# Layer 4 of a fused four-layer graph network: 244 edge tiles without gathers in place of 148, the new ones three nodes wide in three PSUM banks

## What is computed

```python
edge_index = jnp.stack([src, dst])
...
h = jnp.maximum(_layernorm(x, axis=-1), 0.0)
x = x + _L2_gnn_ref(h, edge_index, L2_gnn_Wp, ...)
h = jnp.maximum(_layernorm(x, axis=-1), 0.0)
x = x + _L3_gnn_ref(h, L3_gnn_weight, L3_gnn_loop_weight, edge_weight1, src, dst, edge_type_8)
...
def _L3_gnn_ref(feat, weight, loop_weight, norm, src, dst, etypes):
    all_h = jnp.einsum('ni,rio->rno', feat, weight)
    msg = all_h[etypes, src] * norm
    h = jax.ops.segment_sum(msg, dst, num_segments=feat.shape[0])
    return h + feat @ loop_weight
```

## Time and profile before

| | us |
|---|---|
| median of 3 executions | 6198.45 (6195.6 to 6209.36) |
| profiled execution | 6148.6 |
| its span, first to last instruction | 6146.8 |
| PE busy in the span | 3852.7 (63%) |
| POOL busy | 3724.3 (61%) |
| DVE busy | 2867.0 (47%) |
| ACT busy | 1417.4 (23%) |

### The profile page before, as it was taken

One profiled execution on the slowest core, in us unless ns is written; L12 is line 12 of the kernel. 1 busy time (PEld: TensorE's weight loads), 2 busy tenths in 40 slices (PEclk: granted clock), 3 DMA queues, 4 the chain that ended last, 5 costly groups with the idle time before them and its releaser, 6 DMA issues.

```text
span 6146.8 us, 69225 instructions
## 1 busy us (share of the span) xinstructions
PE 3852.7 (63%) x20719; PEld 3015.9 (49%) x20719; DVE 2867.0 (47%) x9736; ACT 1417.4 (23%) x5476; POOL 3724.3 (61%) x3922
## 2 busy tenths in 40 slices
PE   4889999565555555555555588867466565565433
PEld 3455665454545545455544466634344444444332
DVE  7777776554545455555555533334322322222222
ACT  5333443332223233333333201122000000000000
POOL 4344443566666666666666466645666666666665
PEclk7799999766667677777777799979777777776666
DMA  3233443544444444444444455544111111111121
GB/s 110 95 117 132 145 142 116 157 136 139 137 136 142 135 137 140 146 139 139 138 150 137 147 201 204 192 142 178 47 46 47 46 47 46 46 46 46 47 62 47
DMA packets 310272, 707.07 MB, mean 115 GB/s; under 512 B 72641, under 2 KB 155293, under 8 KB 297613
## 3 DMA queue, kind: packets, MB, share of 16 engines
q0 software_dynamic: 159184, 377.89, 21.4%
q1 hardware_dynamic: 148700, 323.81, 15.2%
q10 hardware_dynamic: 2016, 0.92, 0.1%
HBM read 571.29 MB, written 131.05 MB: 114 GB/s over the span
## 4 chain that ended last, share of the span: by engine, by line
PE 32%; another core or an unknown queue 28%; DVE 19%; issue 15%; ACT 3%; DVEq 1%; DMA 1%; SPq 1%; ACTq 0%
PE ps L2586 11%; DVE oneh L1875 6%; PE ps L2542 4%; DVE ps L2010 3%; PE ps L2571 3%; PE ps L2481 3%; PE ps L2609 3%; PE ps L2493 2%; PE ps L2549 2%; DVE third L2002 2%; PE ps L2431 1%; DVE tmp L1966 1%; ACT h L1644 1%; PE ps L2545 1%
## 5 line engine op out<-in xcount | busy, mean ns | idle before, releaser
L1482 POOL DMA_INDIRECT rows<-tab_rel,third x1299 | 1251.0, 963 | 625.8 <-issue 371.8
L1482 POOL DMA_INDIRECT rows<-tab_hp,idx_src x1120 | 1083.4, 967 | 546.3 <-issue 310.5
L1482 POOL DMA_INDIRECT rows<-tab_h,idx_src x810 | 783.8, 968 | 777.0 <-PE ps L2549 432.5
L2609 PE MATMUL ps<-third 128*128 128x128 f32 x3126 | 618.8, 359 | 666.1 <-issue 416.8
L2586 PE MATMUL ps<-third,h 128*120 128x385 bf16 (+20 forms) x4606 | 875.8, 337 | 68.2 <-issue 29.8
L2609 PEld LDWEIGHTS ps<-third 128*128 128x128 f32 x3126 | 551.8, 264 | 721.4 <-issue 453.1
L2542 PE MATMUL ps<-oneh,rows 128*128 128x128 f32 x2598 | 484.6, 339 | 597.5 <-DVE oneh L1875 301.9
L2542 PEld LDWEIGHTS ps<-oneh,rows 128*128 128x128 f32 x2598 | 428.8, 244 | 682.5 <-issue 347.5
L2586 PEld LDWEIGHTS ps<-third,h 128*120 128x120 bf16 (+10 forms) x4606 | 588.2, 131 | 286.0 <-issue 59.3
L1693 ACT ACTIVATE turned_words<-turned_words 128x128 f32<-128x128 f32 x1563 | 463.1, 298 | 1117.3 <-DVE turned_words L2015 874.5
L1482 POOL DMA_INDIRECT third<-tab_hp,idx_src x443 | 430.2, 971 | 229.2 <-issue 120.8
(11 more groups left out here) (285 smaller groups left out, 5123.1 us busy)
## 6 DMA issues: line engine op xcount, KB each, us to landing
third<-dst_flat SPq DMA_DIRECT2D x390, 256.0 KB
h<-cnt_d SPq DMA_DIRECT2D x48, 1568.0 KB
cnt_d<-h SPq DMA_DIRECT2D x46, 1568.0 KB
tab_rel<-third SPq DMA_DIRECT2D x49, 512.0 KB
rows<-tab_rel,third POOLq DMA_INDIRECT x1299
rows<-tab_hp,idx_src POOLq DMA_INDIRECT x1120
rows<-tab_h,idx_src POOLq DMA_INDIRECT x810
third<-tab_hp,idx_src POOLq DMA_INDIRECT x443
```

The lines of the kernel that those rows point to most:

```text
L1482: pool.indirect_dma_start(out=to[:, t, 0:n], out_offset=None, in_=table[:, :], in_offset=bass.IndirectOffsetOnAxis(ap=idx[:, col:col + 1], ...
L2609: last = pe.matmul(ps_t[sl][:, t * P:(t + 1) * P], onehT[:, sl, t * P:(t + 1) * P], pwin[:, st["v"] % 2, :], start=True, stop=True)
```

## The change

The dense part takes 96 tiles more, 148 to 243, in packs of one tile. Their window is three nodes wide: `pairs3` has 49x3x8 = 1176 columns, `count3` makes three matmuls (408, 408, 360 columns) into three banks, which rotate over banks 0 to 3, and five packs (15 slots, 120 columns) make a bundle. So there are 20 bundles more, 33 in all. The heads move behind, to tiles 244 to 359 (still 116 gathers, but 26 heads), and the tiles gathered from `tab_rel` are 360 to 1562: 1203 in 301 turns. Each bank's eviction is signalled alone, and a count waits for its own bank only. The keys' rows stand in another part of SBUF. `WIN3` becomes a width per pack.

```diff
-PACKS3 = ((4, 36), (2, 76), (1, 148))
-WIN3, SLOTS3, NQ3 = 2, 16, 3
+PACKS3 = ((4, 36, 2), (2, 76, 2), (1, 148, 2), (1, 244, 3))
+SLOTS3, NQ3 = 16, 3
...
-HEAD_END, HEAD_WIN, HEAD_SPAN, HEAD_BATCH = 66, 16, 11, 4
+HEAD_END, HEAD_WIN, HEAD_SPAN, HEAD_BATCH = 90, 16, 11, 4
...
+    bundles3 = []
+    while not bundles3 or bundles3[-1][-1] < len(packs3) - 1:
+        k0 = bundles3[-1][-1] + 1 if bundles3 else 0
+        w = packs3[k0][2]
+        bundles3.append([k for k in range(k0, min(len(packs3), k0 + SLOTS3 // w)) if packs3[k][2] == w])
...
+                            n_banks = -(-nb * w // 512)
+                            per_bank = -(-nb // n_banks)
+                            parts = []
+                            for q0 in range(0, nb, per_bank):
+                                bank = next(bank_at) % 4
+                                parts.append((bank, q0, min(nb, q0 + per_bank), n_cev3.get(bank, 0)))
...
-                pack_cost = 1.1 * (nt3 * 1700.0 + len(bundles3) * (nb * 400.0 + 2000.0))
+                pack_cost = 1.1 * (sum((t1 - t0) * 850.0 * w for t0, t1, w in win3_runs) + len(bundles3) * (nb * 400.0 + 2000.0))
...
-                    for b, (q0, q1) in enumerate(((0, st["half"]), (st["half"], nb))):
-                        last = act.copy(weights3[:, q0:q1, st["place"]:st["place"] + w3],
-                                        ps[st["bank"] + b][:, 0:(q1 - q0) * w3].rearrange("p (q c) -> p q c", c=w3))
-                    last.then_inc(s_cev3.handle, 1)
+                    w = st["w"]
+                    for bank, q0, q1, _ in st["parts"]:
+                        act.copy(weights3[:, q0:q1, st["place"]:st["place"] + w],
+                                 ps[bank][:, 0:(q1 - q0) * w].rearrange("p (q c) -> p q c", c=w)).then_inc(s_cev3.handle, 1)
...
-                    if st["free"]:
-                        pe.wait_ge(s_cev3.handle, st["free"])
-                    for b, (q0, q1) in enumerate(((0, st["half"]), (st["half"], nb))):
-                        last = pe.matmul(ps[st["bank"] + b][:, 0:(q1 - q0) * w3], srow3[:, slot, :],
-                                         pairs3[:, slot, q0 * w3:q1 * w3], start=st["start"], stop=st["stop"])
+                    w = st["w"]
+                    for bank, q0, q1, evicted in st["parts"]:
+                        if st["start"] and evicted:
+                            pe.wait_ge(s_cev3.handle, evicted)
+                        last = pe.matmul(ps[bank][:, 0:(q1 - q0) * w], srow3[:, slot, :],
+                                         pairs3[:, slot, q0 * w:q1 * w], start=st["start"], stop=st["stop"])
```

More of the change, by code:

```diff
@@ L138, in gnn_program @@
                 if u == 0 or forms[u - 1] != forms[u]]
-    packs3 = [(t, n) for k, (n, end) in enumerate(PACKS3) for t in range(PACKS3[k - 1][1] if k else 0, end, n)]
-    pack3_of = {t0 + j: k for k, (t0, n) in enumerate(packs3) for j in range(n)}
-    per3 = SLOTS3 // WIN3
-    bundles3 = [list(range(k, min(len(packs3), k + per3))) for k in range(0, len(packs3), per3)]
-    w3 = WIN3 * n_rel
+    packs3 = [(t, n, w) for k, (n, end, w) in enumerate(PACKS3) for t in range(PACKS3[k - 1][1] if k else 0, end, n)]
+    pack3_of = {t0 + j: k for k, (t0, n, w) in enumerate(packs3) for j in range(n)}
+    bundles3 = []
[3 more added lines that the diff above has]
+        bundles3.append([k for k in range(k0, min(len(packs3), k0 + SLOTS3 // w)) if packs3[k][2] == w])
+    bundle3_of = {k: u for u, members in enumerate(bundles3) for k in members}
+    win3 = [packs3[members[0]][2] for members in bundles3]
+    win3_runs = []
+    for k, (n, end, w) in enumerate(PACKS3):
+        if win3_runs and win3_runs[-1][2] == w:
+            win3_runs[-1] = (win3_runs[-1][0], end, w)
+        else:
+            win3_runs.append((PACKS3[k - 1][1] if k else 0, end, w))
+    w3 = max(win3) * n_rel
+    col3 = nth + 4
+    total3 = col3 + len(bundles3)
+    assert total3 < 512
     full_tiles = n_edges // P
@@ L2197, in vector_keys3_rows @@
             k = t = 0
-            for n, end in PACKS3:
+            for n, end, _ in PACKS3:
                 m = (end - t) // n
@@ L2243, in vector_keys3_keys @@
             idx, u_rel, u_blk, u_row = (tmp_words[:, k * nt3:(k + 1) * nt3].bitcast(U32) for k in range(4))
-            f_rel, f_blk, f_key, f_in = (tmp_words[:, k * nt3:(k + 1) * nt3] for k in range(4, 8))
+            f_rel, f_blk, f_key, f_in = (tmp_words[:, k * nt3:(k + 1) * nt3] for k in (4, 5, 0, 1))
             dve.wait_ge(s_idx3.handle, 16)
@@ L2467, in tensor_program @@
                     for u, members in enumerate(bundles3):
-                        n = len(members) * WIN3
-                        last = pe.matmul(ps[3][0:n, 320 + u:321 + u], first_col[:, u * SLOTS3:u * SLOTS3 + n], ones[0:1, 0:1],
+                        n = len(members) * win3[u]
+                        last = pe.matmul(ps[3][0:n, col3 + u:col3 + u + 1], first_col[:, u * SLOTS3:u * SLOTS3 + n], ones[0:1, 0:1],
                                          start=True, stop=True)
@@ L2473, in tensor_program @@
                     pe.wait_ge(s_key3.handle, st["rows"] + 3)
-                    pe.matmul(ps[3][:, 384:385], ones[:, :], n_inside3[:, :], start=True, stop=True).then_inc(s_key3T.handle, 1)
+                    pe.matmul(ps[3][:, total3:total3 + 1], ones[:, :], n_inside3[:, :], start=True, stop=True).then_inc(s_key3T.handle, 1)
                 elif kind == "count3":
```

78 lines of the change are left out of this document (45 added, 33 removed).

## The result

The changed kernel takes 6164.11 us (median of six executions, 6158.85 to 6177.85); the kernel before, on the same chip, 6202.86. The ratio is 0.9942, 95% interval 0.9931 to 0.9954: 0.6% or 36 us faster (28 to 43); the plain medians lie 39 us apart. The prediction was 6144 us with a range of 6070 to 6360.

A forecast was written before the change was run, and what follows sets the result against it. Layer 4 was taken to run at its gathers' pace, 1.433 us each. 6148.6 - 137.6 (96 gathers) + 58 (X) + 13 + 2 (keys) + 10 (heads) = 6094; plus 49.9 from profile to median, 6144 us; range 6070 to 6360.

The forecast's parts named there:

- the sign: Layer 4's dense part after the change: 1.47 to 1.52 us per gather, clock over 0.85, PE about 85% busy.
- The keys' rows: Small DVE operations that PE and layer 3's gathers wait for: +13 us, all taken as on the path.
- the heads: 13 more adds and three more batches before layer 4's gathers: +10 us, between 0 and 24.
- X: What the new dense work costs layer 4's gathers: +58 us, from 872 gathers at 1.5 us in place of 1.433.
- a bundle has 29.4 us of such work in 37.9: Dense part: PE's full-rate work per bundle, 29.4 us, fits in 37.9 us of gathers; 78% overall.
- Rival B: PE becomes the dense part's bound and the change costs time: 6232 or 6362 us, X from 112 on; chance 0.35.
- sparse stretches: Within the products, single PE instructions 0.70 us apart with nothing to wait for; 8.9 us idle per bundle, 293 for 33.
- Rival A: PE's added work costs the gathers nothing, X under 20: 6091 us, or 6061 with keys and heads hidden; chance 0.18.
- the factor of 1.45: PE's busy time over its full-rate work in the old dense part, 811.0 us for 561, at clock 0.74.
- C: The effects cancel: X between 100 and 125, time 6186 to 6211 us; chance 0.09.
- D: Tiles that don't fit their three nodes start the general loop; left out, as none of 148 to 243 spans more.
- by its rate of instructions: Bound for X from the matmul instruction rate of 3600 to 3900: 7314/5.12 = 1429 us, +179.

The follow-up runs named there:

- pairs_other_form: Changed kernel with DVE writing each pair matrix by scalar_tensor_tensor in place of tensor_scalar: 6183.42 us, ratio 0.9968 to the kernel before, first chip (before about 6203 us).
- three_together: Changed kernel with pairs_other_form's instruction, two-node windows to tile 196 and batched keys' rows: 6137.74 us, ratio 0.9891 to the kernel before, first chip.
- few_products: Changed kernel whose 20 new bundles do 2 of their 49 products each: 5391.6 us, ratio 0.9863 to the kernel before, second chip (before 5461 to 5467 us).
- tiles_248: Changed kernel with 100 new tiles in place of 96, filling the last bundle: 5392.01 us, ratio 0.9865 to the kernel before, second chip.
- two_nodes_to_196: Changed kernel with the first 48 new tiles two nodes wide in two banks, not three: 5373.49 us, ratio 0.9831 to the kernel before, second chip.

## Why the prediction came out as it did

**The direction and the main terms were right.** 1203 gathers, the dense part at 1.50 to 1.53 us per gather (1.47 to 1.52 was named as the sign), clock 0.95 for "over 0.85", PE 86% busy for 85%. The keys' rows cost 13.1 us for 13; the heads 6 for 10, within 0 to 24; the restructuring nothing.

**X was mis-sized: 58 in the sum, 87 by the trace.** With 87 and 6 in their places the sum gives -30 in place of -54; the measured ratio says 36, with 28 to 43 as the interval. The 58 was a choice between bounds, from the pace of another stage, and named no mechanism of its own, so that it came near 87 is partly luck. POOL's longer waits for PE alone are 75. A second cost, the 28 us of longer issues, the prediction put at nothing. It asked of DVE only whether it would be late, with 100 us more of pair matrices, and it wasn't. But while such an operation runs, POOL's issue beside it is longer, and POOL's issue is the pace itself. The rows for it stood there: the issues have a mean of 927.98/958 = 0.969 us in the dense part of the first trace, and a minimum of 0.938. The Trainium skill has the mechanism ("SBUF — State Buffer", section "SBUF: two separate sides"): VectorE and GpSimd share a pair of ports, which a VectorE operation in a two-port mode holds for the whole instruction, and while it does GpSimd can't write the descriptors of a DMA that it issues. The runs agree for the fast form in that issues are longer beside it (0.15 to 0.16 us each beside a long operation, none beside none); that the form runs in a two-port mode, and that the ports are the cause, no run here shows. The page counts an operation with two inputs in SBUF as a holder only against GpSimd work that reads SBUF; pairs_other_form has such an operation, and the issues beside it are 0.26 us longer. The gathers' offsets lie in SBUF (`third`), so they may be such work.

**The part of X that is PE's.** On the first chip POOL waits 75 us longer for PE, and less work for PE takes 41 us of the wait away (three_together). There the prediction's reasoning stands, an amount of work against the time per bundle. On the second chip, with less time per bundle (1.31 us per gather in place of 1.43), there is none of it: few_products gains nothing. So the sentence "a bundle has 29.4 us of such work in 37.9" wasn't wrong, PE does fit on average. Why it is late at times on the first chip is known in part. Rival B's sparse stretches can't be the growth, for they shrank. Idle time of PE before the products (the last column), before and after on the first chip, then the same two on the second (the third row has 12 of the 13 bundles):

```profile
L2493 PE MATMUL ps<-acc,h 128*128 128x128 f32 (+1 forms) x1274 | 227.7, 328 | 163.0 <-issue 112.1
```

```profile
L2528 PE MATMUL ps<-acc,h 128*128 128x120 f32 (+3 forms) x3234 | 438.5, 290 | 76.0 <-issue 46.4
```

```profile
L2493 PE MATMUL ps<-acc,h 128*128 128x128 f32 x1176 | 185.2, 323 | 2.9 <-ACT acc L1657 2.9
```

```profile
L2528 PE MATMUL ps<-acc,h 128*128 128x120 f32 (+3 forms) x3234 | 394.1, 279 | 22.7 <-ACT acc L1683 21.3
```

"issue", idle time that the trace gives no reason for, was 112.1 us in 13 bundles and is 46.4 in 33, 8.6 us and 1.4 us each, where rival B kept 8.9. Of POOL's 107.0 us of waits for PE, about 46 fall in ten places where the granted clock was 0.78 or less over the wait and the 12 us ahead of it: PE stood idle (8.9 us until 5579.25, shown below), or worked without a break at a clock of 0.50 (before those at 4968.93 and 5718.38). In the rest PE was mostly busy at 0.87 to 1.00. What starts each of these is not shown. One place after, where they cost most:

```profile
5567.50 2.83 PE L2516 MATMUL ps<-third 128*128 128x408 f32 x8
...
5575.24 0.95 POOL L1507 DMA_INDIRECT rows<-tab_rel,third  x1 [0.30 <-issue]
5578.54 0.26 ACT L1689 COPY wsum<-ps 128x120 f32<-128x120 f32 x1 [27.44 <-remote]
5578.61 0.29 DVE L1945 TENSOR_SCALAR third<-iota_b,turned_words 128x128 f32<-128x128 f32 x1 [14.49 <-remote]
...
5579.25 0.50 PEld L2516 LDWEIGHTS ps<-third 128*128 128x128 f32 x2 [9.57 <-ACT acc L1683]
...
5586.56 0.94 POOL L1507 DMA_INDIRECT rows<-tab_rel,third  x1 [10.37 <-PE ps L2577]
```

PE's counts start at 5567.50. POOL issues on until its ring is full (5575.24). ACT, whose eviction the next count waits for, and DVE both start again at 5578.5, within 0.1 us of each other, after idle times that the trace gives to no engine of this core ("remote"). PE follows at 5579.25, and POOL has lost 10.37 us. ACT and DVE stood still while POOL issued and moved on when it had stopped, PE behind them. It isn't one place alone: in layer 4 after, ACT or DVE go on 89 times after more than 3 us of "remote", and 51 of these fall in a pause of POOL of over 0.6 us or the 0.3 us behind it, though such pauses are 16% of the time. So the stalls go together with POOL's pauses and with the sessions that have them, as in the earlier trace rows; which causes which, and what is fetched or signalled so slowly, was not found.

**Rival A** (PE costs nothing) is what the second chip shows for PE, though X is not under 20 there: 96 gathers of 1.264 are worth 121 us, DVE's 35 come off, and the stage is 86 us shorter (1641.3 to 1555.6); it begins 15.5 us later, by keys and heads. **Rival B** (PE becomes the bound) took place nowhere: its premise was that the factor of 1.45 stays, and PE's clock rose to 0.95 and 1.00. PE is busy 1157 us in the dense part (4359.9 to 5728.6) for the 971 reckoned, a factor of 1.19. The Trainium skill's rule on cycling through PSUM banks, cited for B ("TensorE: Matmul & The Clock Gate", section "A second HAM failure mode: psum-queue depth-cycling"), is told of a bf16 kernel and is not borne out in this one, with fp32 and three of four banks per tile: the clock was 1.00 over 1062 us on the second chip and 0.95 over 770 on the first. **C** and **D** didn't occur. That the lone pack of the last bundle would matter was thought of only after the result, and tiles_248 shows that it doesn't.

**Slips in the working.** The count of matmuls ahead of the prediction, and the prediction with it, takes the old tiles' 592 for matmuls where they are instructions (148 tiles of two matmuls, each two instructions). So the changed kernel has 584 matmuls of counts and not 880, 3361 in all from the first count to the last product and not 3657, which makes 6722 instructions; the trace after has 6730 in that stretch. The bound for X "by its rate of instructions" is then 6722/5.12 = 1313, +63 us and not +179, and its 5.38 instructions per us lie near the 5.30 of 300 to 1050. With the right count the choice of 58 would have stood between the bounds by pace (+45) and by rate (+63), with the measured 87 above either. The sum of PE's work, 971 us, counted the tiles rightly. And the 330.6 us of idle time before the scatters were read as waits for rows and one-hots, where 199.0 of them are "issue" and only 130.0 one-hots. The expectations have two counts wrong: few_products has 940 matmuls fewer and not 893, and two_nodes_to_196 has 48 matmuls of counts fewer on balance and not 72.

**Open.** What makes the two kinds of session: chip number 0 stands on record with 6204 us and, in a later session, with 5461, so if the number is one chip each time, the pauses and stalls are not the chip's. Further, why an issue is held 0.08 us beside a matrix of 0.69 us on the second chip (0.12 on the first) and 0.15 where some are of 0.89; whether the hold grows with an operation's length or faster; and PE's part of X on the first chip, which few_products would test and which wasn't run there. The -30 us of the corrected sum and the measured -36 differ by what one profile of each kernel can't tell.

## To carry to other kernels

Where a stream of DMAs issued by GpSimd is the pace, read the mean duration of one issue beside its minimum, by stretch, and charge long VectorE operations to that stream too: here 96 matrices of 0.89 us came with 28 to 35 us more of issuing, on a VectorE that was 36% busy. Take the narrowest window that the data allow (two nodes to tile 196 gave 16 us) before adding work of any kind beside such a stream. And small bookkeeping that a later stage waits for (some 190 operations on one partition, 27 us on DVE) can lie on the path: batching it gave 12 us by the medians.

## What the runs showed of the hardware

The same kernel takes 6203 us in one session and 5464 in another, and most of the difference is in the pauses between gathers: 584 us of "remote" waits against none, 197.9 of them in layer 4. In the same sessions there are sparse stretches of PE's instructions (112.1 us of idle time without a shown reason before the products of the kernel before) against none. A change is worth different things on the two, 0.9942 and 0.9859. PE held a granted clock of 1.00, the upper of its two levels (2.4 GHz), for 1062 us at 93% busy; with few_products, 82% busy, it was 0.89. An indirect DMA's issue takes 0.94 us alone and 1.45 and 1.67 us in the two places shown beside a long VectorE operation.
